# ScalarE issues the writes of the signs of layer 1 and six early loads of layer 3 that SyncE issued

## The reference

```python
def _L1_conv_ref(x, W):
    xb = ste_sign(x)
    wb = ste_sign(W)
    return lax.conv_general_dilated(xb, wb, (1, 1), [(1, 1), (1, 1)], dimension_numbers=('NCHW', 'OIHW', 'NCHW'))

x = x + _L0_conv_ref(_gn(x), ...)
x = x + _L1_conv_ref(_gn(x), L1_conv_W)
x = x + _L2_conv_ref(_gn(x), ...)
x = x + _L3_conv_ref(_gn(x), ...)
```

## Time and profile before

| | us |
|---|---|
| median of 3 runs (4338.14 to 4343.95) | 4339.41 |
| the profiled execution, its own time | 4362.16 |
| its span in the trace | 4360.3 |
| PE busy | 3266.8 (75%) |
| DVE, ACT, POOL busy | 2071.6, 1784.8, 1956.4 |
| chain that ended last: PE, DMA, SP's issues | 42%, 24%, 11% |
| mean granted clock of TensorE, as a share of full speed | 0.898 |

### The profile page before, as it was taken

How to read it: one execution, slowest core, us unless ns; L and a number is a source line. 1 busy time by engine, 2 the same in 40 slices (tenths; PEclk the granted TensorE clock), 3 DMA queues, 4 the chain that set the end, 5 groups by cost and what they waited for, 6 DMA issues and landing times.

```text
span 4360.3 us, 70554 instructions
## 1 busy us (share of the span) xinstructions
PE 3266.8 (75%) x26592; PEld 2091.4 (48%) x26592; DVE 2071.6 (48%) x6038; ACT 1784.8 (41%) x2626; POOL 1956.4 (45%) x3175
## 2 busy tenths in 40 slices
PE   0676987769876787777886787866877769777698
PEld 0443545435454454544455454553545536445355
DVE  2627643266432754337543384424744257432573
ACT  2443633336343463435434354343542436424232
POOL 1326544265433654346442564326543265332754
PEclk9988998889988898888988899988999889888899
DMA  6388697876969669596786967869778697786946
GB/s 210 58 149 169 147 318 198 155 163 153 337 166 176 163 184 327 130 213 143 198 299 123 212 153 219 288 106 211 148 227 280 105 209 159 236 268 106 205 79 218
DMA packets 589273, 829.51 MB, mean 190 GB/s; under 512 B 489731, under 2 KB 490502, under 8 KB 572550
## 3 DMA queue, kind: packets, MB, share of 16 engines
q1 hardware_dynamic: 323200, 734.28, 66.4%
q10 hardware_dynamic: 216582, 76.68, 8.2%
q0 software_dynamic: 49152, 14.05, 2.1%
HBM read 375.89 MB, written 267.45 MB: 148 GB/s over the span
## 4 chain that ended last, share of the span: by engine, by line
PE 42%; DMA 24%; SPq 11%; DVE 8%; ACT 5%; ACTq 4%; POOL 4%; issue 3%; DVEq 0%; POOLq 0%
PE acc L979 24%; PE acc L996 12%; SPq L327 9%; DMA arena<-x 6%; DMA out<-y 6%; DMA dense_out<-arena 5%; POOL y L510 3%; DMA arena<-signs 3%; PE acc L1058 3%; ACT arena L599 2%; ACTq L606 2%; DMA signs<-arena 2%; ACTq L535 2%; DVE dense_stats L860 1%; DMA arena<-y 1%
## 5 line engine op out<-in xcount | busy, mean ns | idle before, releaser
L979 PE MATMUL acc<-y,arena 64*128 64x384 f32 x9216 | 1726.5, 501 | 179.9 <-ACT y L568 146.1
L979 PEld LDWEIGHTS acc<-y,arena 64*128 64x128 f32 x9216 | 1014.0, 194 | 739.2 <-ACT y L568 230.6
L327 POOL DMA_DIRECT2D arena<-y x1536 | 790.6, 522 | 836.7 <-PE acc L996 725.4
L996 PE MATMUL acc<-arena 64*128 64x384 f32 x4608 | 958.4, 509 | 226.3 <-issue 208.9
L568 ACT ACTIVATE y<-acc 128x768 f32<-128x768 f32 x832 | 644.4, 808 | 1177.0 <-PE acc L996 1176.1
L489 POOL TENSOR_SCALAR arena<-arena,cst,fill 128x24 f32<-128x24 f32 (+1 forms) x1536 | 613.7, 419 | 710.7 <-issue 469.8
L510 POOL TENSOR_TENSOR y<-arena,y 128x3072 f32<-128x3072 f16 x88 | 529.9, 6045 | 735.0 <-DMA arena<-dense_out 734.9
L860 DVE BATCH_NORM_STATS2 dense_stats<-y 128x6 f32<-128x192 f32 x1536 | 408.0, 344 | 729.2 <-POOL y L510 728.9
L996 PEld LDWEIGHTS acc<-arena 64*128 64x128 f32 x4608 | 525.1, 196 | 450.7 <-issue 240.9
L1058 PE MATMUL acc<-arena,wd_side 128*32 128x384 fp8e4 (+1 forms) x10752 | 471.8, 330 | 287.1 <-DMA arena<-signs 234.6
L802 DVE TENSOR_SCALAR_CACHE_REDUCE y<-acc 128x768 f32<-128x768 f32 x256 | 245.1, 958 | 640.3 <-PE acc L996 640.3
(11 more groups left out here) (86 smaller groups left out, 1287.1 us busy)
## 6 DMA issues: line engine op xcount, KB each, us to landing
y<-x SPq DMA_DIRECT2D x64, 2304.0 KB, 27.1
out<-y SPq DMA_DIRECT2D x64, 2304.0 KB, 22.9
arena<-y SPq DMA_DIRECT2D x768, 141.0 KB
arena<-x SPq DMA_DIRECT2D x168, 576.0 KB, 6.5
dense_out<-arena ACTq DMA_DIRECT2D x384, 192.0 KB, 7.0
arena<-dense_out SPq DMA_DIRECT2D x192, 384.0 KB, 7.0
arena<-y SPq DMA_DIRECT2D x768, 71.9 KB
arena<-signs SPq DMA_DIRECT2D x192, 250.0 KB, 10.3
```

Source lines behind the costliest of these rows:

```text
L327: eng.dma_start(halo[at:at + n, slot, :, d0:d0 + size], y[source:source + (n - 1) * step + 1:step, first + odd:first + odd + 3:2, s0:s0 + ...
L979: nc.tensor.matmul(acc[:, 2 * k + odd, 0:KN], w_center[at, slot, 2 * q + odd, :], y[at, 2 * g + odd, k * KN:(k + 1) * KN], start=turn == 0 ...
L996: nc.tensor.matmul(acc[:, 2 * k + odd, 0:KN], w_halo[at, slot, q, :], halo[at, bt % HALO_SLOTS, q, k * KN:(k + 1) * KN], start=False, stop ...
```

## The change

In layer 1 the writes of the signs leave SP's program. ScalarE issues them itself, directly behind the last signs of the batch, after a wait for its own signs to be written (`sign_ready`). The buffer in HBM is now declared with half as many elements of two bytes, and the transfers to and from it are described in elements of two bytes; the bytes are the same.

In layer 4 the six early loads with i = 18 to 23 leave SP's program. ScalarE issues load 18+g itself behind the two passes over channel 16+g, for g from 0 to 5, after a wait for its own second pass. The early loads 0 to 17 stay on SP, where they were.

```diff
-        signs = nc.dram_tensor("signs", [P, C, STAGED], F8, kind="Internal").ap()
+        signs = nc.dram_tensor("signs", [P, C, STAGED // 2], F16, kind="Internal").ap()
...
+        def ahead_channel(eng, s, i):
+
+            eng.dma_start(ahead[:, i % AHEAD_SLOTS, :], x[s + 1, :, AHEAD_FIRST + i].rearrange("p g w -> p (g w)"))\
+                .then_inc(ahead_in[i % AHEAD_SLOTS], 16)
...
-            def write_signs(s, b):
-                sp.wait_ge(sign_ready, s * PAIRS + (b + 1) * BATCH_PAIRS)
-                src = stage_bytes[:, (b % 2) * STAGE_BYTES:(b % 2) * STAGE_BYTES + BATCH_CH * STAGED]
-                for a in range(2):
-                    to = signs[a * 64:(a + 1) * 64, b * BATCH_CH:(b + 1) * BATCH_CH, :]
-                    sp.dma_start(to.rearrange("(i j) c n -> j i (c n)", j=S), src[a:P:2, :])\
-                        .then_inc(sign_out[b % 2], 16)
...
                         sp.dma_start(
-                            sign_in[w % 2][q:q + 32, 0:SUBS * PLANE].rearrange("p (u n) -> p u n", u=SUBS),
-                            signs[p2:p2 + 63:2, :, w * WROWS * PITCH:w * WROWS * PITCH + PLANE]
+                            sign_pairs[w % 2][q:q + 32, 0:SUBS * PLANE // 2].rearrange("p (u n) -> p u n", u=SUBS),
+                            signs[p2:p2 + 63:2, :, w * WROWS * PITCH // 2:(w * WROWS * PITCH + PLANE) // 2]
                             .rearrange("u c n -> c u n")).then_inc(sign_loaded[w % 2], 16)
...
                     if b + HALO_SLOTS < BATCHES:
                         halos(first + b + HALO_SLOTS)
-                    if b > 0:
-                        write_signs(s, b - 1)
-                write_signs(s, BATCHES - 1)
...
                         halos(first + b + HALO_SLOTS)
-                    for i in range(2):
-                        load_ahead(s, PAIRS + AHEAD_SLOTS + 2 * b + i)
                     store(s, b)
...
                 last.then_inc(sign_ready, 1)
+                if g % BATCH_PAIRS == BATCH_PAIRS - 1:
+                    act.wait_ge(sign_ready, s * PAIRS + g + 1)
+                    first = A_STAGE + (b % 2) * STAGE_BYTES
+                    src = part(first, STAGE_BYTES, F16)[:, 0:BATCH_CH * STAGED // 2]
+                    for a in range(2):
+                        to = signs[a * 64:(a + 1) * 64, b * BATCH_CH:(b + 1) * BATCH_CH, :]
+                        act.dma_start(to.rearrange("(i j) c n -> j i (c n)", j=S), src[a:P:2, :])\
+                            .then_inc(sign_out[b % 2], 16)
...
                             ahead_stats(s, PAIRS + g)
+                            if PAIRS + g + AHEAD_SLOTS < AHEAD:
+                                act.wait_ge(act_stat, stat_count(act_channels, s, 0) + PAIRS + g + 1)
+                                ahead_channel(act, s, PAIRS + g + AHEAD_SLOTS)
```

More of the change, by code:

```diff
@@ L250, in conv_preact_kernel @@
         sign_in = [part(A_SIGN + k * SIGN_BYTES, SIGN_BYTES, F8) for k in range(2)]
+        sign_pairs = [part(A_SIGN + k * SIGN_BYTES, SIGN_BYTES, F16) for k in range(2)]
         d_stage = part(A_DSTAGE, SUBS * WN * 2, F16).rearrange("p (u n) -> p u n", u=SUBS)
@@ L371, in load_ahead @@
             def load_ahead(s, i):
-                if s < B - 1 and i < AHEAD:
+                if s < B - 1:
                     if i >= AHEAD_SLOTS:
                         sp.wait_ge(act_stat, stat_count(act_channels, s, 0) + i - AHEAD_SLOTS + 1)
-                    sp.dma_start(ahead[:, i % AHEAD_SLOTS, :], x[s + 1, :, AHEAD_FIRST + i].rearrange("p g w -> p (g w)"))\
-                        .then_inc(ahead_in[i % AHEAD_SLOTS], 16)
-            def write_signs(s, b):
-                sp.wait_ge(sign_ready, s * PAIRS + (b + 1) * BATCH_PAIRS)
-                src = stage_bytes[:, (b % 2) * STAGE_BYTES:(b % 2) * STAGE_BYTES + BATCH_CH * STAGED]
-                for a in range(2):
-                    to = signs[a * 64:(a + 1) * 64, b * BATCH_CH:(b + 1) * BATCH_CH, :]
-                    sp.dma_start(to.rearrange("(i j) c n -> j i (c n)", j=S), src[a:P:2, :])\
-                        .then_inc(sign_out[b % 2], 16)
+                    ahead_channel(sp, s, i)
             def load_signs(s, w):
```

## The result

The changed kernel takes 4363.49 us (median of 6 runs, 4353.97 to 4372.34), the kernel before beside it 4338.77 us (6 runs). The ratio is 1.0054, with a 95% interval of 1.0031 to 1.0076: **25 us slower**, where 43 us faster was forecast and the range ended at 4345.

The account below looks back on a forecast made before the run. It took the DMA engines to bound the 132 us from layer 4's first store. Terms of 1.8 + 3.7 + 1.2 + 1.5 - 2.0 = 6.2 us, seven times, 43 us, turned 4339.41 into 4296 us; range 4235 to 4345.

Parts of the forecast that it names:

- (b): Layer 4: early loads 18 and 19 leave the DMA-bound stretch for the room before it; gain 3.7 us per sample change.
- (c): Layer 4: the second store and the load behind it come earlier, without loads 20 and 21 ahead; gain 1.2 us.
- (f): Layer 1: writes of batches 0 and 1 now run beside last store, last load and batch 3's halo copies; loss 2.0 us.
- (g): ScalarE's issuing of writes and loads hides in its idle time, and SP's lost waits held back nothing needed; costed at nothing.
- (a): Head of layer 4's store stretch: the first store no longer stands behind two early loads; gain 1.8 us.
- (e): Layer 1: batch 0's signs are written earlier and ScalarE's 22.47 us wait vanishes; gain taken as 1.5 us.
- (d): Layer 4: TensorE's 16.5 us of waits from early loads go, but return as halo waits in its second half; nothing gained.
- (h): Sign buffer transfers described in two-byte elements: same bytes in the same contiguous runs; taken as nothing.
- rival 2: Sample changes: only issue time is saved, 3.0 us less 2.0 for the early writes, seven times; 4332 us, chance 0.16.
- Rival 3: Layer 1: slower, because ScalarE's issues of a write outlast its 2.61 us gap; 4360 us at 3.6 us a pair, chance 0.12.

## Why the prediction was wrong, step by step

**Two things failed: (b) with (c), which made the forecast a gain, and (f) with the last sentence of (g), which made the result a loss.** From 43 us faster to 25 us slower are 68 us. Steps (a) to (c) were to bring 7 x 6.7 = 47 us; the kernel with only the loads moved is at 0.9991, the one with only the elements at 0.9992, so they brought nothing. Steps (e), (f) and (g) were to cost 7 x 0.5 = 3.5 us; between 0.9991 and 1.0054 are 27 us.

**(b) and (c)** forecast 4.9 us of B. B is 149.1 us in the changed kernel and 147.5 with the writes on SP, where the two kernels with the old order have 148.3 and 146.7: nothing came of it. The mean share of 0.96 over 132 us was read as a bound by bytes everywhere in the stretch. Right behind loads 18 and 19 the share was 0.81 already (mean of seven changes), since the second store wasn't there yet, and taking these loads away only widened that gap. And loads 20 to 23, whose move was costed at a gain, cost more on ScalarE's queue than they won: left on SP they give 0.9954 in place of 0.9991.

**(f)** took 2.0 us for two early writes, from their bytes, and held that the first "may cost nothing" since at 3348 most engines are dry (0.48). By the ratios the early writes with what follows from them cost 30 us, 4.3 a change. The 0.48 was a mean over 17 us and over 16 engines. In the kernel before, the windows ahead of the last store's landing at 3360 read (the last two columns are DMA's share and GB/s):

```profile
3344.00:3348.00 4.00, 4.00 (x25) 3.35 (x22) 2.00 (x6) 3.46 (x6) 0.00 (x0) 0.91 1.00 363
3348.00:3352.00 4.00, 4.00 (x30) 2.88 (x28) 1.71 (x3) 1.36 (x5) 0.00 (x0) 1.00 0.69 276
3352.00:3356.00 4.00, 2.52 (x18) 1.70 (x14) 1.72 (x6) 2.10 (x2) 1.32 (x4) 1.00 0.14 58
3356.00:3360.00 4.00, 1.99 (x8) 1.43 (x10) 0.62 (x1) 0.00 (x0) 3.90 (x10) 0.80 0.11 40
```

At 3348 the engines weren't dry: the share is 1.00 just ahead and 0.69 just behind. In the changed kernel the write of batch 0 goes out at 3353.92, into this:

```profile
3353.00:3357.00 4.00, 4.00 (x30) 3.09 (x28) 1.53 (x4) 1.02 (x2) 0.00 (x0) 1.00 0.93 352
```

In the kernel before, from 3352 on, a share of 0.14 and 0.11 is about two engines of 16, and the store has not landed while they work. That an early write delays just those is a guess: the trace doesn't name the engines, and the last store takes no longer in the changed kernel. The surer part of the loss was in no term at all: the end of **(g)** had costed the waits that SP loses at nothing ("halo copies that nothing was short of"). They spaced the copies of batch 5 from those of batch 3, for which TensorE stood, and putting a wait back there took the time from 1.0054 to 0.9989.

The other steps:

- (a) was right: A fell by 2.1 us, 1.8 forecast.
- (d) was right that most of the 16.5 us would not be won, wrong on where they go: TensorE's waits for evictions at the head of layer 4 fell to 7.9 us in the sixth change, not to nothing, 5.7 us came back behind VectorE, and the waits for borders in the rest of layer 4, where they were to show, stayed (11.2 us before, 10.4 now).
- (e) forecast 1.5 us; D fell by 0.4. Covered by the same standstill; its worth shows only in the kernels with the copies moved.
- (g), but for its last sentence, and (h) were right: two issues fit in ScalarE's 2.61 us, and the elements do nothing. The sign given for it, idle time near 1.4 us, was a misreading: the 2.61 us of such a row contain the issues.

Two of the prediction's own signs point the same way. The 15 us ahead of the first store had a share of 0.50 in the sixth change, above 0.42, so the two loads did move into the room; and the time from the first store to the last one's landing stayed at 149 us, which it had named as the sign of rival 2. Rival 2, "only issue time is saved", is nearer to the loads than the forecast, though even its 3.0 us a change didn't show in the ratio; and it, too, put (f) at 2.0. Rival 3 had the sign right and the mechanism wrong. Of the 25 us lost, 7 x 2.8 = 20 are in the table's sums; with one execution for each, that is no closer than the 22.8 us by which the one of the kernel before was over its median.

The Trainium skill, DMA: Bandwidth & Descriptors, "Issuing engines are not separate DMA queues", says that another engine's transfers share the same DMA engines and that only issue time is saved. The runs agree as far as they can tell: loads 18 and 19 alone brought 0.9954 against 0.9992, 16 us, where step (a), the issue time, is 7 x 1.8 = 13 us; the 16 us are known to some 12 us either way. For 20 to 23 they show less than issue time saved, with the stores' landing at 25.8 us beside 22.9.

## What to carry to other kernels

A queue also spaces and orders: before moving a transfer off it, ask what its place there held back, and which transfer of the critical chain it will now run beside. Read a DMA share as a mean over time and over engines: 0.96 over 132 us held a gap that got wider when bytes left it, and 0.48 over 17 us was 1.00 first and 0.11 last, with a store still under way that SP waited for. A wait under a longer wait can be worth nothing until the longer one goes; here the fix for the longer one alone was 0.7% slower, both together 0.7% faster.

## What the runs showed of the hardware that I had not expected

- The same early load takes 3.7 to 3.9 us on ScalarE's queue while the engines have room and 10.4 to 19.1 us once stores are under way. On SP's queue, at the same changes, it took 6.0 to 10.9 us for the first four and 15.4 to 18.6 for the last two: a second queue gains where the engines have room and not in the backlog.
- A write of signs doubled, 0.64 MB more beside the halo copies, cost nothing that could be measured, while an extra one some 20 us earlier cost 0.0026 of the time, 11 us in all, with intervals that just touch. Why the moment should matter, and how copies issued later on one queue can delay those ahead of them, stays open: no row shows the single engines.
